# Gate logits of a fused attention and feed-forward layer: split products against plain float32 in four column strips

## What is computed

```python
h = layernorm(x)                                  # (32, 128, 512)
logits = jnp.einsum('bsh,he->bse', h, gate_w)     # gate_w is (512, 8)
routing_weights, _ = jax.lax.top_k(logits, 2)
shared = jnp.einsum('bsi,ih->bsh', jnp.square(relu(h @ up_w)), down_w)   # 512 -> 2048 -> 512
moe = (h @ expert_weight) * routing_weights.sum(-1, keepdims=True)
y = layernorm(shared + moe) * ln_gamma + ln_beta
out = x + tanh(g_ffn) * y
```

## Time and profile before

| | |
|---|---|
| median of three runs | 1330.37 us (1329.75 to 1331.53) |
| profiled execution, its own time | 1329.5 us |
| its span | 1327.3 us |
| TensorE matmuls busy | 1295.6 us, 98% of the span |
| VectorE / ScalarE / GpSimd busy | 72% / 44% / 39% |
| granted TensorE clock, mean | 0.994 |
| gate matmuls (L1672, L1675) | 8 in each of 8 groups |
| turning matmuls (L1683) | 4 in each of 8 groups, 8 records |

### The profile page before, as it was taken

How to read it: one execution, slowest core, us unless ns; L and a number is a source line. 1 busy time by engine, 2 the same in 40 slices (tenths; PEclk the granted TensorE clock), 3 DMA queues, 4 the chain that set the end, 5 groups by cost and what they waited for, 6 DMA issues and landing times.

```text
span 1327.3 us, 27876 instructions
## 1 busy us (share of the span) xinstructions
PE 1295.6 (98%) x8924; PEld 1110.7 (84%) x8924; DVE 954.8 (72%) x1824; ACT 585.0 (44%) x1835; POOL 518.1 (39%) x671
## 2 busy tenths in 40 slices
PE   6999999999999998999999999999999999999997
PEld 4788888888888886888888888888888888888886
DVE  5677777777777767785776776776776776776765
ACT  4778877788777785322123123223222222212121
POOL 2566666666658874350240240240240240240121
PEclk9999999999999999999999999999999999999999
DMA  6389888898988844458368368368368377367532
GB/s 240 88 207 227 230 232 220 222 223 231 232 202 200 201 112 148 138 135 262 122 178 246 117 177 241 119 182 244 115 180 246 112 184 246 109 182 225 173 133 63
DMA packets 403226, 243.71 MB, mean 184 GB/s; under 512 B 303576, under 2 KB 303704, under 8 KB 403160
## 3 DMA queue, kind: packets, MB, share of 16 engines
q1 hardware_dynamic: 370520, 183.63, 52.4%
q10 hardware_dynamic: 32640, 59.26, 13.5%
HBM read 178.60 MB, written 64.23 MB: 183 GB/s over the span
## 4 chain that ended last, share of the span: by engine, by line
PE 82%; issue 8%; DVE 5%; POOL 2%; ACT 1%; DMA 1%; ACTq 0%; SPq 0%; DVEq 0%; POOLq 0%
PE bank L76 17%; PE bank L78 16%; PE bank L77 16%; PE wide L77 7%; PE wide L78 7%; PE wide L76 7%; PE bank L406 4%; PE wide L394 3%; PE bank L415 2%; DMA prob<-in_wk 1%; DVE c L1478 1%; POOL yrstd L1976 1%; DVE yst L1855 1%; PE wide L1675 0%; DMA wo_lo<-ring_scratch 0%
## 5 line engine op out<-in xcount | busy, mean ns | idle before, releaser
L1749 ACT ACTIVATE hT_hi<-c 128x512 fp32r<-128x512 f32 x128 | 79.9, 631 | 408.6 <-PE wide L78 217.5
L1983 POOL TENSOR_TENSOR pair<-pair,beta 128x512 f32<-128x512 f32 x28 | 38.2, 1364 | 455.2 <-DMA pair<-x_scratch 455.2
L77 PE MATMUL wide<-wo_lo,hT_hi 128*128 128x512 f32 x512 | 203.6, 398 | 0.0
L78 PE MATMUL wide<-wo_hi,hT_lo 128*128 128x512 f32 x512 | 202.3, 395 | 0.0
L76 PE MATMUL wide<-wo_hi,hT_hi 128*128 128x512 f32 x512 | 201.9, 394 | 0.0
L784 ACT ACTIVATE prob<-wide,nmx 128x128 f32<-128x128 f32 x512 | 182.2, 412 | 2.5 <-DVE nmx L595 2.5
L961 POOL TENSOR_TENSOR prob<-prob,rr 128x512 f32<-128x512 f32 x128 | 133.9, 1052 | 75.0 <-DVE rr L603 75.0
L1829 DVE TENSOR_TENSOR hT_lo<-c,hT_hi 128x512 fp32r<-128x512 f32 x128 | 99.5, 797 | 78.6 <-ACT hT_hi L1749 78.1
L784 ACT ACTIVATION_READ_ACCUMULATOR prob<-wide,nmx 128x1 f32 x512 | 129.7, 253 | 0.0
L78 PEld LDWEIGHTS wide<-wo_hi,hT_lo 128*128 128x128 f32 x512 | 96.4, 188 | 22.7
L76 PEld LDWEIGHTS wide<-wo_hi,hT_hi 128*128 128x128 f32 x512 | 96.5, 188 | 21.6
(11 more groups left out here) (234 smaller groups left out, 3480.1 us busy)
## 6 DMA issues: line engine op xcount, KB each, us to landing
wo_hi<-ring_scratch ACTq DMA_DIRECT2D x110, 256.0 KB, 3.7
wo_lo<-ring_scratch ACTq DMA_DIRECT2D x110, 256.0 KB, 4.7
wo_hi<-ring_scratch SPq DMA_DIRECT2D x46, 256.0 KB, 2.9
wo_lo<-ring_scratch SPq DMA_DIRECT2D x46, 256.0 KB, 3.2
xin<-in_x SPq DMA_DIRECT2D x32, 256.0 KB, 3.3
cin<-in_ctxT SPq DMA_DIRECT2D x32, 256.0 KB, 2.9
xres<-in_x SPq DMA_DIRECT2D x32, 256.0 KB, 3.7
x_scratch<-x SPq DMA_DIRECT2D x32, 256.0 KB, 3.1
```

The costliest lines, as they stand in the source:

```text
L77: eng.matmul(dst, ah, bl, start=False, stop=False)
L78: mm = eng.matmul(dst, al, bh, start=False, stop=last and k == n - 1)
L1749: return act.activation(dst, src, ACT.Copy)
```

## The change

The gate is computed by plain float32 matmuls. The stationary tile is the whole gate weight of a 128-row slice, padded with zeros to 32 columns; the moving tile is 128 tokens of `xT_hi` or of `xT_lo`. Each of the four token tiles writes its own strip of 32 output partitions: 4 slices by 2 parts by 4 tiles are 32 matmuls a group in place of 8. ACT copies 128 x 128 in place of 16 x 512. One 128 x 128 transpose takes the place of the four turning matmuls. The split of the gate weights on ACT and DVE and the load of the doubled identity go; a memset of `ga` on POOL at the start of the kernel comes, and SP waits for it before it loads the gate weights into the first 8 of each 32 columns (32-byte pieces).

```diff
@@ attention half: DVE slot, ACT slot, POOL before
-                    if is_slot(s, NB - 3):
-                        ff.split_gate_lo(dve)
...
-                    if is_slot(s, NB - 3):
-                        ff.split_gate_hi(act)
...
+                    ff.zero_gate(pool)
@@ feed_forward_start
-    ga = sb("ga", [P, KT, 2, NE], F32R)
...
-    two_ident = sb("two_ident", [2 * NE, NE])
+    ga = sb("ga", [P, KT, P // GB])
...
-    lg = sb("lg", [2 * NE, D])
+    lg = sb("lg", [P, P])
...
-            sp.dma_start(ga_raw[:, :, :], t["gate"].rearrange("p (k n) -> p k n", k=KT)).then_inc(ld_g, DMA)
-            sp.dma_start(two_ident[:, :], t["two_ident"]).then_inc(ld_g, DMA)
+            sp.wait_ge(ga_zeroed, 1)
+            sp.dma_start(ga[:, :, 0:NE], t["gate"].rearrange("p (k n) -> p k n", k=KT)).then_inc(ld_g, DMA)
...
-    def split_gate_hi(act):
-        act.wait_ge(ld_g, 4 * DMA)
-        act.activation(ga_hi, ga_raw[:, :, :], ACT.Copy).then_inc(ga_split, 1)
...
+    def zero_gate(pool):
+        pool.memset(ga[:, :, :], 0.0).then_inc(ga_zeroed, 1)
@@ gate
             for k in range(KT):
-                pe.matmul(BG[0:2 * NE, :], ff.ga[:, k, :, :].rearrange("p x n -> p (x n)"), ff.xT_hi[:, k, :],
-                          start=k == 0, stop=False)
-            for k in range(KT):
-                mm = pe.matmul(BG[0:NE, :], ff.ga_hi[:, k, :], ff.xT_lo[:, k, :], start=False, stop=k == KT - 1)
+                for m, xT in enumerate((ff.xT_hi, ff.xT_lo)):
+                    for j in range(GB):
+                        strip = slice(j * (P // GB), (j + 1) * (P // GB))
+                        mm = pe.matmul(BG[strip, 0:P], ff.ga[:, k, :], xT[:, k, j * P:(j + 1) * P].bitcast(F32),
+                                       start=k == 0 and m == 0, stop=k == KT - 1 and m == 1)
@@ turn_logits
-            for j in range(GB):
-                mm = pe.matmul(BTG[:, j * NE:(j + 1) * NE], ff.lg[:, j * P:(j + 1) * P], ff.two_ident[:, :],
-                               start=True, stop=True)
-            mm.then_inc(ff.pe_TG, 1)
+            pe.transpose(BTG[:, 0:P], ff.lg[:, :], ident[:, :]).then_inc(ff.pe_TG, 1)
@@ group (PE), logits (ACT), routing (DVE)
-                        pe.wait_ge(ff.ga_done, 1)
+                        pe.wait_ge(ff.ld_g, 3 * DMA)
...
-            copy(ff.lg[:, :], bank[1][0:2 * NE, :]).then_inc(ff.ac_G, 1)
+            copy(ff.lg[:, :], bank[1][:, 0:P]).then_inc(ff.ac_G, 1)
...
-                i = dve.max(top[:, j, :], bank[2][:, j * NE:(j + 1) * NE])
+                i = dve.max(top[:, j, :], bank[2][:, j * (P // GB):j * (P // GB) + NE])
```

More of the change, by code:

```diff
@@ L1072, in feed_forward_start @@
     gamma, beta = sb("gamma", [P, D]), sb("beta", [P, D])
-    ga = sb("ga", [P, KT, 2, NE], F32R)
-    ga_hi, ga_lo = ga[:, :, 0, :], ga[:, :, 1, :]
-    ga_raw = sb("ga_raw", [P, KT, NE])
-    two_ident = sb("two_ident", [2 * NE, NE])
+    ga = sb("ga", [P, KT, P // GB])
     hT_hi = [sb(f"hT_hi{n}", [P, D], F32R) for n in range(2)]
@@ L1106, in feed_forward_start @@
     uh, ul, us, usl, qh, ql = (sem("f_" + n) for n in ("uh", "ul", "us", "usl", "qh", "ql"))
-    fcst, ld_g, ga_split, ga_done = (sem("f_" + n) for n in ("consts", "ld_g", "ga_split", "ga_done"))
+    fcst, ld_g, ga_zeroed = (sem("f_" + n) for n in ("consts", "ld_g", "ga_zeroed"))
     ld_x = [sem(f"fld_x{n}") for n in range(GB)]
@@ L1410, in inv_std @@
         pool.tensor_tensor(rstd[:, :], var[:, :], powers[:, 0:1], ALU.pow).then_inc(po_rs, 1)
-    def split_gate_hi(act):
-        act.wait_ge(ld_g, 4 * DMA)
-        act.activation(ga_hi, ga_raw[:, :, :], ACT.Copy).then_inc(ga_split, 1)
-    def split_gate_lo(dve):
-        dve.wait_ge(ga_split, 1)
-        dve.tensor_tensor(ga_lo, ga_raw[:, :, :], ga_hi.bitcast(F32), ALU.subtract).then_inc(ga_done, 1)
+    def zero_gate(pool):
+        pool.memset(ga[:, :, :], 0.0).then_inc(ga_zeroed, 1)
     def prepare(dve):
-        dve.wait_ge(ld_g, 4 * DMA)
+        dve.wait_ge(ld_g, 3 * DMA)
         dve.tensor_scalar(gamma[:, :], gamma[:, :], tanh_g[:, 1:2], None, ALU.mult).then_inc(fcst, 1)
@@ L1498, in feed_forward_start @@
     start.po_r, start.po_t, start.po_ys, start.po_yv = po_r, po_t, po_ys, po_yv
-    start.st_n, start.st_o, start.ld_r, start.ld_t, start.fcst, start.ga_done = st_n, st_o, ld_r, ld_t, fcst, ga_done
-    start.ga, start.ga_hi, start.ga_lo, start.two_ident, start.gamma, start.beta, start.lg = (
-        ga, ga_hi, ga_lo, two_ident, gamma, beta, lg)
+    start.st_n, start.st_o, start.ld_r, start.ld_t, start.fcst, start.ld_g = st_n, st_o, ld_r, ld_t, fcst, ld_g
+    start.ga, start.gamma, start.beta, start.lg = ga, gamma, beta, lg
     start.hT_hi, start.hT_lo, start.xT_hi, start.xT_lo, start.xn, start.y, start.pair = (
@@ L1507, in feed_forward_start @@
     start.ring_first, start.quarters = ring_first, quarters
-    start.split_gate_hi, start.split_gate_lo, start.load_first, start.load_piece, start.load_x = (
-        split_gate_hi, split_gate_lo, load_first, load_piece, load_x)
+    start.zero_gate, start.load_first, start.load_piece, start.load_x = zero_gate, load_first, load_piece, load_x
     return start
```

## The result

The changed kernel takes 1321.61 us (median of six runs, 1319.54 to 1324.35), the kernel before 1330.30 us beside it. The ratio is 0.9931 with a 95% interval of 0.9905 to 0.9957; six more runs on another occasion gave 0.9933 (0.9920 to 0.9945). So it is faster by about 9 us. The forecast was 1324.1 us, and its best case was 1322.1 with some tenths for scatter.

A forecast was written before the change was run, and what follows sets the result against it. The prediction took TensorE's row of matmuls plus a few waits as the bound. Its terms, -1.4 - 2.4 - 1.9 - 0.6 = -6.3 us, gave 1323.2 from the profiled execution, 1324.1 us against the median; range 1322.1 to 1330.4 with some tenths for scatter.

The forecast's parts named there:

- The gate, +0.33: Gate matmuls on TensorE: 2.18 us a group against 1.85, so 0.33 us dearer, bounds +0.17 and +0.49.
- The turning, -0.93: Turning of the logits on TensorE: one transpose at 0.25 us against 1.18, bounds -1.06 and -0.80 a group.
- Group 0, -3.8: First feed-forward group: -1.4 us from an earlier end of the turning and -2.4 us from a clock that stays up.
- The first term: Group 0: turning starts 0.32 us earlier after a smaller copy, first product behind it comes earlier, -1.4 us.
- The second step: Group 0: standstill shrinks from 2.48 to 1.83 us, so the clock stays at 2.4 GHz, -2.4 us, bounds 0 and -2.7.
- Groups 1 to 6, -1.9: Middle groups: +0.33 for the gate, -0.65 for the residual load landing earlier, six times; bounds +2.0 and -3.6.
- rival 2: Middle groups: residual load's chain takes the turning's gain; 1328.0 us with clock kept (chance 0.12), 1330.4 with it lost (0.14).
- Group 7, -0.6: Last group: DVE has 0.73 us idle in q = 2 and can follow most of the way, -0.6 us.
- Small things, costed at nothing: Memset on POOL, dropped weight split on ACT and DVE, SP's issue and wait, 32-byte DMA pieces: priced at nothing.
- Rival 1: Group 0: the clock still falls behind the standstill; 1326.5 us in all, chance 0.24.
- Rival 3: Gate: strips overlap less than the values' strips; without overlap 0.15 us a record, near 1380 us; chance 0.10.
- Rival 4: Nothing measurable, since TensorE's list does not end a group; rival 2 with the clock lost, 1330.4 us, chance 0.14.

The follow-up runs named there:

- after_shift: The changed kernel with 160 unused bytes a partition ahead of the hidden tiles, so moved tiles stand as in the kernel before modulo 256: 1323.53 us, ratio 0.9954.
- before_shift: The kernel before with 96 unused bytes a partition ahead of the hidden tiles and nothing else changed: 1326.71 us, ratio 0.9984.
- before_ahead: The kernel before with SP issuing the awaited residual load ahead of the store, for q = 2 and 3: 1325.71 us, ratio 0.9968.
- shift_ahead: after_shift with SP issuing the awaited residual load ahead of the store, for q = 2 and 3: 1317.48 us, ratio 0.9907.
- strips_serial: The changed kernel with the gate's 32 products ordered strip by strip, all eight of one strip before the next: 1345.96 us in one run.

## Why the forecast was right, and where it failed

**The gate, +0.33.** Measured +0.22, inside the bounds. A record took 29.4 ns, not the values' 31.6, and way in and out 0.09 and 0.10 instead of 0.05 and 0.11. The Trainium skill, "TensorEngine Tiling (Array Packing)", Key Properties, says that a change of tiling mode drains TensorE and gives no price. The trace agrees that the change costs something, about 0.1 us on either side, less than the 0.16 that I had taken as the bound for a full drain.

**The turning, -0.93.** Measured -1.07, just beyond the bound of -1.06 that I had put as the best case: the transpose starts an ordinary step of 0.12 us after the product ahead of it and the next product 0.03 us later.

**Group 0, -3.8.** The stretch from gate to gate gave -5.4 with the new places and -4.5 without (104.49 in after_shift). The first term came as forecast in size, 1.4 us: 0.3 by a shorter standstill, 0.1 by the gate and 1.0 by the turning itself. The standstill shrank by 0.31 us and not by 0.65, because the gate is not longer in this group: from its start to the last product ahead of the turning are 5.53 us, before 5.62. The second step, "So I take it that the clock stays up", failed as a mechanism: at 2.16 to 2.19 us eight of nine fell. The 2.4 us came nevertheless, in another way, and that is luck: a shorter stretch at 1.2 GHz (1.3 to 1.6 us lost, not 2.8), waits that absorb part of it, and the wait for the weight load at 614 us gone, which I had left standing.

**Groups 1 to 6, -1.9.** The chain was read rightly in its links: from the issue of the residual load to POOL's addition are 9.9 us on the mean of the six groups, before 10.7, so 0.8 less (I took 0.65, at most 0.93), and the waits grew. But its start was not fixed. `result` of tile 0 stands at 15.7 us after the gate in all six groups before; in the changed kernel it does so in three (15.5 to 15.7), and in the other three it comes at 16.4 to 16.8 us. These are the three in which TensorE had waited for the routing, a wait that the forecast did not have. Group 3 shows it, with its gate at 824.16 us (TensorE, then DVE):

```profile
833.49 0.47 PE L76 MATMUL wide<-wo_hi,hT_hi 128*128 128x512 f32 x1 [0.49 <-DVE route L1824]
840.91 0.74 DVE L1853 SCALAR_TENSOR_TENSOR fy<-fy,yrstd,pair 128x512 f32<-128x512 f32 x1
```

Against the gate, the addition so came only 0.3 us earlier on the mean. How much the chain takes varies between executions of the changed lists: the waits in the middle groups of the changed kernel were 3.6 and 4.5 us in two profiles, and 5.6 in after_shift, whose middle groups gained nothing at all (595.26 against 594.78). That is rival 2 in one execution. In the changed kernel the 5.2 us of its middle groups, less the 2.4 to 3.6 by which the places shorten the lists (waits taken off: before to before_shift, after_shift to the changed kernel), leave 1.6 to 2.8, near the forecast's 1.9. Between before_ahead and shift_ahead, where nothing is taken, the whole change is worth 0.61% or 8.1 us, 2 more than with the chain.

**Group 7, -0.6.** Measured -0.7.

**Small things, costed at nothing: the step that failed.** I priced the memset, the split, the DMA pieces, and looked at which instructions the resized tiles need; I did not ask what they push along. 1536 `downward` matmuls 5 ns faster, 2000 up matmuls 1.7 ns slower on the mean and an attention half 1.3 us longer are -7.7 + 3.4 + 1.3 = -3.0 us. Measured are -2.1 in before_shift and, between after_shift and the changed kernel, -3.1. So this is the step that failed: the move of the tiles stood at nothing and was worth 2 to 3 us. With the tiles held in place the change gives 0.9954, 6.1 us, near the forecast's 6.3; that the agreement is so close is partly luck, since the clock's term came by another way. The range was summed from the bounds of the terms I had, and had no room for one that I had not.

**Rivals.** Rival 1 was true of eight profiles of nine in its event (the clock falls) and false in its price. Rival 2 was true of a part. Rival 3's mechanism shows in strips_serial, but the order of the loops keeps clear of it by a factor of three. Rival 4 did not occur.

## To carry to other kernels

When a change resizes any buffer, write down where every tile behind it moves to, and compare the steps of untouched matmuls first; a control with unused bytes costs one line, tells placement from mechanism, and is itself worth trying as an improvement. One profile cannot tell whether a standstill keeps the clock: look at several, or fill it. Where one queue carries a store and an awaited load that become ready together, issue the load first.

## What the runs showed of the hardware that I had not expected

- The start of a stationary tile within 256 bytes, with the moving operands at 224, changes the step of full-array products by 2 to 3%: 228 ns at 224 against 233 at 0 and 128 for 512 columns, 116.8 to 120.0 for 256. The best place differs between the two kinds, and the cause is open.
- A standstill of 2.16 to 2.19 us kept the clock in one profile and lost it in eight; one of 2.47 us kept it.
- The 64 records of the gate cost 29.4 ns each when neighbours lie in different strips and 92 ns when they don't.
- A 256 KB load issued 0.84 us behind a store of the same size on the same queue was there 3.0 us later, counted from its issue, than one issued ahead of it. The Trainium skill, "DMA: Bandwidth & Descriptors", Queues, rings and completion order, says that each DMA engine takes the descriptors of one issuing engine's queue in ring order; the two timelines of SP and POOL agree.
